# Turning residual tokens through VectorE and HBM instead of TensorE, with LayerNorm rows moved between the query's high parts

## What is computed

```python
# block 1: group norm, 1x1 convolutions to q, k, v, softmax attention, projection, residual
xn = group_norm(x); q, k, v = split(qkv_w @ xn + qkv_b)
x1 = x + proj_w @ (softmax(q^T k / sqrt(C)) applied to v) + proj_b
# block 2: on tokens t (N x C), LayerNorm, rows of length one, squared cosines, softmax
t  = tokens(x1);  z = layer_norm(t)
zn = z / |z|;     t = t + softmax((zn zn^T)^2) z
# block 3: LayerNorm, sign weights, clip to [-1, 1], seven levels, residual, back to channels
y  = layer_norm(t) @ (sign(W - mean W) * mean|W|) + b
out = channels(t + round(clip(y, -1, 1) * 7) / 7)
```

## Time and profile before

| | |
|---|---|
| Time, median of 3 runs | 1728.92 (1728.91, 1728.92, 1734.53) |
| Profiled execution, device time | 1734.94 |
| Its span | 1733.2 |
| Granted TensorE clock, mean | 0.995 |
| Busy: TensorE / VectorE / ScalarE / GpSimd | 96% / 79% / 57% / 45% |
| DMA queue of SyncE | 259.48 MB, 49.1% of 16 engines |

### The profile page before, as it was taken

One profiled execution on the slowest core, in us unless ns is written; L12 is line 12 of the kernel. 1 busy time (PEld: TensorE's weight loads), 2 busy tenths in 40 slices (PEclk: granted clock), 3 DMA queues, 4 the chain that ended last, 5 costly groups with the idle time before them and its releaser, 6 DMA issues.

```text
span 1733.2 us, 33604 instructions
## 1 busy us (share of the span) xinstructions
PE 1659.1 (96%) x10994; PEld 1509.8 (87%) x10994; DVE 1369.7 (79%) x2687; ACT 988.5 (57%) x1586; POOL 771.9 (45%) x1206
## 2 busy tenths in 40 slices
PE   7999999999999999999999999999999999999996
PEld 6897889988898898888988898898988989899886
DVE  6778688797877978788787887978778787887865
ACT  3455655656566565655657556565655656565572
POOL 1262634726345353543626346253553635337161
PEclk9999999999999999999999999999999999999998
DMA  4544546355454554545445463554545545463442
GB/s 127 163 121 155 147 140 194 117 170 151 148 173 130 184 146 155 145 148 186 140 153 155 143 190 112 179 154 148 162 141 174 159 139 154 149 188 103 161 132 61
DMA packets 218750, 259.86 MB, mean 150 GB/s; under 512 B 30176, under 2 KB 188256, under 8 KB 218720
## 3 DMA queue, kind: packets, MB, share of 16 engines
q1 hardware_dynamic: 218720, 259.48, 49.1%
HBM read 138.81 MB, written 120.59 MB: 150 GB/s over the span
## 4 chain that ended last, share of the span: by engine, by line
issue 24%; PE 18%; POOL 17%; DMA 15%; DVE 11%; ACT 7%; SPq 6%; POOLq 1%; DVEq 0%; ACTq 0%
DMA e_scratch<-x_norm 11%; PE wide L465 10%; SPq L392 6%; POOL e_back L1485 4%; ACT ln L863 4%; POOL prob L1480 3%; DMA e_back<-e_scratch 3%; PE turn L679 3%; POOL xn_lo L1436 2%; PE narrow L465 2%; POOL ln_r L1446 2%; DVE prob L1139 2%; DVE prob L1115 2%; POOL val L1472 2%; DVE neg_max L1125 1%
## 5 line engine op out<-in xcount | busy, mean ns | idle before, releaser
L465 PE MATMUL wide<-xn_hi,prob 128*128 128x512 f32 x1024 | 302.0, 399 | 21.2 <-DVE prob L1115 21.2
L822 ACT ACTIVATE expo<-wide,neg_max 128x1024 f32<-128x1024 f32 x128 | 142.7, 1114 | 199.4 <-DVE neg_max L1125 198.2
L465 PEld LDWEIGHTS wide<-xn_hi,prob 128*128 128x128 f32 x1024 | 187.3, 189 | 64.3 <-DVE prob L1115 24.5
L1496 POOL TENSOR_TENSOR carrier_p<-ones 128x1 f32<-128x1 f32 x60 | 15.7, 261 | 398.1 <-DVE y_sb L1241 395.6
L1139 DVE TENSOR_TENSOR prob<-e_back,prob 128x1024 fp32r<-128x1024 f32 x112 | 135.9, 1213 | 56.3 <-ACT prob L829 56.3
L1134 DVE STREAM_TRANSPOSE x_norm<-expo 128x1024 f32<-128x1024 f32 x112 | 139.3, 1244 | 44.5 <-ACT expo L822 42.6
L829 ACT ACTIVATE prob<-e_back 128x1024 fp32r<-128x1024 f32 x112 | 118.3, 1056 | 91.7 <-DMA e_back<-e_scratch 91.2
L1480 POOL TENSOR_TENSOR prob<-expo,prob 128x128 fp32r<-128x128 f32 (+6 forms) x112 | 146.2, 1317 | 47.6 <-DVE prob L1174 47.6
L465 PE MATMUL wide<-xn_lo,prob 128*128 128x512 f32 x512 | 161.2, 395 | 0.0
L1125 DVE TENSOR_REDUCE neg_max<-wide 128x1 f32<-128x1024 f32 x128 | 155.2, 1213 | 4.9 <-PE wide L465 3.6
L558 PE MATMUL wide<-prob 128*128 128x256 f32 x512 | 149.6, 292 | 5.0 <-DVE prob L1139 4.9
(11 more groups left out here) (181 smaller groups left out, 5180.7 us busy)
## 6 DMA issues: line engine op xcount, KB each, us to landing
e_scratch<-x_norm SPq DMA_DIRECT2D x112, 512.0 KB, 3.5
e_back<-e_scratch SPq DMA_DIRECT2D x448, 128.0 KB, 2.9
x_raw<-in_x SPq DMA_DIRECT2D x32, 512.0 KB, 3.7
e_back<-in_x SPq DMA_DIRECT2D x64, 256.0 KB, 5.0
out<-y_sb SPq DMA_DIRECT2D x64, 256.0 KB, 3.1
ln_scratch<-x_norm SPq DMA_DIRECT2D x30, 512.0 KB, 3.0
expo<-ln_scratch SPq DMA_DIRECT2D x120, 128.0 KB, 2.8
e_scratch<-x_norm SPq DMA_DIRECT2D x32, 448.0 KB, 2.6
```

What stands on the lines that cost most here:

```text
L465: mm = pe.matmul(o, lhsT, r, start=first and i == 0, stop=last and i == len(parts) - 1)
L822: act.activation(expo[:, n % DEEP], wide[n % 2][:, :], ACT.Exp, bias=neg_max[:, n:n + 1], accum_out=row_sum1[:, n:n + 1]).then_inc(e1_made, 1)
```

## The change

The tokens no longer go through TensorE. VectorE turns their 32 x 32 squares (`tok_turn`, two transposes of 128 x 512 for each half) into the place where the LayerNorm rows were, SyncE writes them to HBM and reads them back (`send_tok`, `fetch_tok`, between the sends and fetches of exponentials 1 and 2), and `output` adds them from SBUF in one instruction for each half. `turn_t` and its waits leave TensorE's front; behind the loop, the last sample keeps them (`output_last`). The bounds of the output move from VectorE (`clip`) to GpSimd (`quantise`). The LayerNorm rows: in `back` ScalarE makes four of the eight, and the other four in `front`, two behind each high part of the query; VectorE turns the first half in `back` and the second behind the first row maximum; GpSimd makes the first coefficients between two bias additions. On VectorE the group norm's sums go ahead of the query's low parts, the turned input tokens (`x_tokens`) behind them, and the low part of the last exponentials and one residual change places with their neighbours.

```diff
+        tok_scratch = nc.dram_tensor("tok_scratch", (2, P, N), F32).ap()
+        tok_in = tok_scratch.rearrange("h (q c) (b f) -> h b c q f", q=SQ, b=SQ)
...
+            def send_tok(f, hf):
+                sp.wait_ge(tok_turned, 2 * f + hf + 1)
+                sp.dma_start(tok_scratch[hf], tok_sent[hf]).then_inc(tok_written[hf], 16)
+            def fetch_tok(f, hf):
+                sp.wait_ge(tok_written[hf], 16 * (f + 1))
+                back = tok_back[hf].rearrange("p (q f) -> p q f", q=SQ)
+                for c in range(SQ):
+                    sp.dma_start(back[c * Q:(c + 1) * Q], tok_in[hf, c]).then_inc(tok_landed[hf], 16)
...
                 for n in range(SENT):
                     send(b, n)
+                    if f is not None and n in (1, 2):
+                        send_tok(f, n - 1)
                     fetch(b, n)
+                    if f is not None and n in (1, 2):
+                        fetch_tok(f, n - 1)
...  (TensorE)
-                if f is not None:
-                    pe.wait_ge(y_made, 4 * f + 4)
-                    turn_t(f, 0)
                 product1(b, 0)
                 scores1(b, 5)
-                if f is not None:
-                    pe.wait_ge(out_made, 2 * f + 1)
-                    turn_t(f, 1)
...  (ScalarE)
                 query_hi(b, 0)
+                if f is not None:
+                    layer_norm2(f, 4)
+                    layer_norm2(f, 5)
                 query_hi(b, 1)
+                if f is not None:
+                    layer_norm2(f, 6)
+                    layer_norm2(f, 7)
                 value_hi(b, 0)
                 value_hi(b, 1)
+                exp1(b, 0)
                 if f is not None:
                     ln2T_hi(f, 0)
-                exp1(b, 0)
...
-                for n in range(NT):
+                for n in range(HT):
                     layer_norm2(b, n)
...  (VectorE)
+            def tok_turn(f, hf):
+                dve.wait_ge(t2_made, NT * f + HT * (hf + 1))
+                dve.wait_ge(pv2_up, NT * f + NT)
+                for k in range(KC):
+                    last = dve.transpose(
+                        tok_sent[hf].rearrange("p (c k n t) -> p k n c t", c=SQ, k=KC, t=Q)[:, k],
+                        tok[:, HT * hf:HT * (hf + 1), tile(k)].rearrange("p n (c t) -> p n c t", t=Q))
+                last.then_inc(tok_turned, 1)
...
+            def output(f, hf):
+                dve.wait_ge(tok_landed[hf], 16 * SQ * (f + 1))
+                dve.wait_ge(q_made, 2 * f + hf + 1)
+                y = y_sb[:, hf].rearrange("p k (q f) -> p k q f", q=SQ)
+                dve.tensor_tensor(y, tok_back[hf].rearrange("p (q k f) -> p k q f", q=SQ, k=KC), y, ALU.add
+                                  ).then_inc(out_made, 1)
...
+                if more:
+                    gn_sums(b + 1, 0)
                 query_lo(b, 0)
+                if more:
+                    gn_sums(b + 1, 1)
+                query_lo(b, 1)
+                value_lo(b, 0)
...
                 x_tokens(b, 0)
-                query_lo(b, 1)
                 x_tokens(b, 1)
-                value_lo(b, 0)
+                row_max(b, 0)
+                if f is not None:
+                    ln2_turn(f, 1)
+                e1_turn(b, 0, f)
                 value_lo(b, 1)
-                if more:
-                    gn_sums(b + 1, 0)
-                row_max(b, 0)
+                row_max(b, 1)
                 if f is not None:
                     ln2T_lo(f, 0)
-                e1_turn(b, 0, f)
-                row_max(b, 1)
-                if more:
-                    gn_sums(b + 1, 1)
+                e1_turn(b, 1, f)
+                if f is not None:
+                    tok_turn(f, 0)
                 value_lo(b, 2)
-                e1_turn(b, 1, f)
                 value_lo(b, 3)
-                if f is not None:
-                    clip(f, 0)
                 row_max(b, 2)
                 if f is not None:
                     ln2T_lo(f, 1)
                 e1_turn(b, 2)
+                if f is not None:
+                    tok_turn(f, 1)
...
-                if f is not None:
-                    clip(f, 1)
...
+                e1T_last_lo(b)
                 e1T_lo(b, 6)
                 residual1(b, 4)
-                e1T_last_lo(b)
+                residual1(b, 5)
                 e2_hi(b, 0)
                 e2_hi(b, 1)
-                residual1(b, 5)
...
-                for hf in range(2):
-                    ln2_turn(b, hf)
+                ln2_turn(b, 0)
...  (GpSimd)
             def quantise(f, hf):
                 i = 2 * f + hf
+                aside(hf, y_made, 2 * i + 2)
+                pool.tensor_scalar(y_sb[:, hf], y_sb[:, hf], 1.0, -1.0, ALU.min, ALU.max).then_inc(clip_made, 1)
...
-                    for g in range(2):
-                        bias_quads(b + 1, g)
-                for g in range(N2):
+                    bias_quads(b + 1, 0)
+                layer_norm2(b, 0)
+                if more:
+                    bias_quads(b + 1, 1)
+                for g in range(1, N2):
                     layer_norm2(b, g)
```

More of the change, by code:

```diff
@@ L142, in build @@
         ln2_back = [expo[:, 2], expo[:, 3]]
+        tok_scratch = nc.dram_tensor("tok_scratch", (2, P, N), F32).ap()
+        tok_in = tok_scratch.rearrange("h (q c) (b f) -> h b c q f", q=SQ, b=SQ)
+        tok_sent = [ln2[:, HT * hf:HT * (hf + 1), :].rearrange("p n c -> p (n c)") for hf in range(2)]
+        tok_back = [tok[:, HT * hf:HT * (hf + 1), :].rearrange("p n c -> p (n c)") for hf in range(2)]
         e2_flat = x_tok[:, :, :].rearrange("p n c -> p (n c)")
@@ L278, in build @@
         ln2_landed = [sem("ln2_landed0"), sem("ln2_landed1")]
+        tok_turned = sem("tok_turned")
+        tok_written = [sem("tok_written0"), sem("tok_written1")]
+        tok_landed = [sem("tok_landed0"), sem("tok_landed1")]
         ln2T_up = sem("ln2T_up")
@@ L682, in ffn, with turn_t @@
                 mm.then_inc(y_up, 1)
-            def turn_t(f, hf, places=PLACES):
+            def turn_t(f, hf, places):
                 for k in range(KC):
@@ L1250, in quantise, with output_last @@
                                   ).then_inc(q_made, 1)
-            def output(f, hf, places=PLACES):
-                dve.wait_ge(tT_up, 2 * f + hf + 1)
+            def output(f, hf):
[4 more added lines that the diff above has]
+                                  ).then_inc(out_made, 1)
+            def output_last(f, hf, places):
+                dve.wait_ge(tT_up, hf + 1)
                 dve.wait_ge(q_made, 2 * f + hf + 1)
@@ L1269, in front @@
                 x_tokens(b, 0)
-                query_lo(b, 1)
                 x_tokens(b, 1)
-                value_lo(b, 0)
-                value_lo(b, 1)
-                if more:
-                    gn_sums(b + 1, 0)
                 row_max(b, 0)
                 if f is not None:
+                    ln2_turn(f, 1)
+                e1_turn(b, 0, f)
+                value_lo(b, 1)
+                row_max(b, 1)
+                if f is not None:
                     ln2T_lo(f, 0)
-                e1_turn(b, 0, f)
-                row_max(b, 1)
-                if more:
-                    gn_sums(b + 1, 1)
+                e1_turn(b, 1, f)
+                if f is not None:
+                    tok_turn(f, 0)
                 value_lo(b, 2)
-                e1_turn(b, 1, f)
                 value_lo(b, 3)
-                if f is not None:
-                    clip(f, 0)
                 row_max(b, 2)
@@ L1390, in _ @@
             quantise(f, 0)
-            output(f, 0, LAST)
+            output_last(f, 0, LAST)
             clip(f, 1)
             quantise(f, 1)
-            output(f, 1, LAST)
+            output_last(f, 1, LAST)
         @block.gpsimd
```

## The result

The changed kernel takes 1820.19 (median of four, 1816.35 to 1822.73) where the kernel before, now with a fourth run, takes 1729.69: a ratio of 1.0512, 95% interval 1.0487 to 1.0538, or 90 microseconds more. The profiled execution takes 1821.66 with a span of 1819.7; the profile of before has a span of 1733.2, so 86.5 are added.

What follows compares the result with a forecast made beforehand. SyncE's queue of dependent sends and fetches of exponentials, ending in T6, was taken to set the period. 0.96 + 3.23 + 0.4 = 4.6 a sample, 15 x 4.6 = 69, gave 1798 against the median 1728.92; range 1757 to 1840.

Steps and rivals of the forecast that it cites:

- second LayerNorm send: SyncE's send of the LayerNorm rows' second half, turned after the first row maximum: 13.9 after Q, now 9.0.
- Q: The start of a sample's queries on TensorE; the period runs from one to the next.
- first send: SyncE's first send of exponentials to HBM in a sample: at 781.8 against 780.84, +0.96.
- six steps: SyncE's queue from first to seventh send of exponentials: +3.23, plus 0.4 for waits on token writes.
- T6: End of VectorE's low part of the seventh turned block; each microsecond it comes late is one of the period.
- T6 - Q: Time from Q to T6 in a sample: to grow by 4.6, to about 65.5.
- rest: Period less T6 - Q, the time from T6 to the next Q: to stay 44.
- I take 0.2 each: Token fetches' waits for their own sends on SyncE's queue: 0.4 a sample, between nothing and 0.93 each.
- The price of the issues: Four more fetches on SyncE's queue in the second and third step each: 2 x 1.85 = 3.70.
- A: Rival: TensorE's work is the bound and gives back 3.06 a sample, 1683; chance 0.08.
- B: Rival: no change, VectorE takes TensorE's place as the bound, about 1729; chance 0.07.
- C: Rival: token trips crowd the DMA engines, 1847, and TensorE's clock falls too, 1871; chance 0.09.

Runs made afterwards that it cites:

- e7_early_second: e2_on_tensor with the second LayerNorm half turned behind the query's low parts, input tokens around the first maximum, exponentials' second low part ahead of the output: 1712.01, ratio 0.9888.
- e9_no_turn: e7_early_second with the tokens turned nowhere, so that the output adds them as they lie: 1739.91, ratio 1.0038.
- e1_no_trip: The changed kernel without the token sends and fetches through HBM and VectorE's wait for them; VectorE still turns the tokens: 1743.75, ratio 1.0084.
- The ladder: Three kernels compared: e1_no_trip 1743.75, e5_small 1771.91, the changed kernel 1820.19.
- e2_on_tensor: The changed kernel with tokens turned on TensorE as before and no trip through HBM; spread LayerNorm rows, new order and GpSimd bounds stay: 1740.11, ratio 1.0061.
- e3_trip_old_order: The changed kernel with LayerNorm rows, GpSimd's coefficients and VectorE's first orders as in the kernel before; the token trip stays: 1787.36, ratio 1.0319.
- e5_small: The changed kernel with every token DMA kept at its place but an eighth of the bytes moved: 1771.91, ratio 1.0241.

## Why the prediction was right, and where its sum was off

The direction, the place and the mechanism held; one term of the sum was too small. Step by step, eighth sample:

| step | forecast | measured |
|---|---|---|
| second LayerNorm send after Q | 13.9 | 13.85 |
| first send after Q | 18.38 | 18.38 |
| step from the first send to the second | 5.42 | 5.21 |
| second to third | 7.27 + 0.2 | 7.30 |
| third to fourth | 7.27 + 0.2 | 8.24 |
| fourth to fifth | 5.42 | 6.25 |
| fifth to seventh | 10.84 | 10.95 |
| six steps | 36.6 | 37.95 |
| seventh send to T6 | 10.43 | 10.36 |
| T6 - Q | 65.5 | 66.69 |
| T6 to the next Q | 44 | 43.88 |

**T6 sets the period.** Of the twelve kernels ten have a rest of 43.9 to 44.1, with T6 - Q from 60.8 to 67.6; the two others are `e7_early_second` and `e9_no_turn`, in which TensorE waits for T6 in two samples or fewer. But the constant rest alone doesn't say that T6 leads. In the kernel before TensorE waits for that low part 3 times, and in `e1_no_trip` 3 times too: there its own chain and T6 run level, and the sentence that a microsecond of T6 is a microsecond of the period holds only from some tenths on (T6 - Q grew by 5.91, the period by 5.77). In the changed kernel TensorE waits 15 times, and in the seven others of the ten in at least eight samples. The saving on TensorE turned into waits, as forecast: for the first scores it waits no more, for VectorE's last low part it waits 1.62.

**The token write was priced in the wrong place.** The step that failed is the one that ends at "I take 0.2 each, near the lower end, since the stretch is not full". The wait for the token's own write costs nothing, because the queue is busy with a fetch while it lands. But the bytes are on the engines when the next sends of exponentials go out: those are written 4.49 - 3.57 = 0.92 and 4.41 - 3.57 = 0.84 later. This is almost the 0.93 that the prediction held as the upper bound, and it fell on the sends behind, one step later each. The first step gave back 0.2, so the six came out 1.3 above the sum. The stretch was indeed not full, but it should have been judged with the new bytes in it. The kernel before, same view as above, in the stretch of its eighth sample that answers to 821 to 841:

```profile
786.00:791.00 5.00, 5.00 (x25) 4.05 (x24) 4.76 (x9) 2.67 (x5) 3.14 (x4) 1.00 0.59 185
791.00:796.00 5.00, 5.00 (x32) 4.36 (x31) 4.15 (x6) 3.49 (x5) 0.00 (x0) 1.00 0.59 191
796.00:801.00 5.00, 5.00 (x33) 4.40 (x32) 4.82 (x8) 2.27 (x3) 4.32 (x7) 1.00 0.55 182
801.00:806.00 5.00, 5.00 (x39) 4.77 (x38) 4.29 (x9) 1.65 (x3) 0.33 (x2) 1.00 0.69 210
```

A mean share of 0.605 is 12.1 of 20 microseconds. The two token halves, written and read, are 2.1 MB, which at the 284 GB/s worked out in the prediction take 7.4 of all engines: an estimate of 19.5 of 20, where the changed kernel then had a mean share of 0.91. That the stretch would be nearly full could be worked out from the trace of before.

**The price of the issues stood, while the bytes were there.** The sum has 3.70 for eight more issues, and in the changed kernel's queue they are all there: 3.70 + 0.92 + 0.84 is 5.46, the 5.4 that the trip costs. The ladder splits the same 5.4 as 2.2 + 3.2, because with few bytes the sends behind the issues are written sooner. So 0.4 for the bytes became 1.8 on top of the issues, and the forecast of 4.1 for the trip became 5.4. With the upper bound taken for the token writes the sum would have been 4.6 - 0.4 + 1.9 = 6.1, where 5.9 was measured. That upper end of the forecast, 1820, is the measured time to the microsecond by luck: the samples give less, and a difference between executions makes up for it.

**From samples to the kernel.** The samples 2 to 15 take 1682.80 - 128.7 = 1554.1 where they took 1473.7: 5.7 each, not 4.6. Over 15 samples that is 17 of the 22 by which the forecast of 1798 fell short. The rest is between executions: the two profiled ones differ by 86.7, the medians by 90.5.

**The rivals.** A (TensorE the bound) and B (VectorE the bound) needed a T6 that comes before TensorE or VectorE wants it, and would have shown in a rest above 44, as in `e7_early_second`; the changed kernel has 43.88. The Trainium skill's rule (Perfetto Trace Analysis, Identifying the Most-Contended Engine), to optimise first the engine with the highest occupancy, speaks for A; the runs disagree twice. With the transposes on TensorE (`e2_on_tensor`, 96%) the time is 1740, without them and without a trip (`e1_no_trip`) 1744; and even at 97% in `e7_early_second`, taking them away made it 1740 from 1712 (with a fall of the clock in it). C had the right mechanism, crowded DMA engines, at too high a price, and its second half did not matter: the clock does fall in the changed kernel (0.983 granted over the span, 0.995 before), but the rest behind T6 stays at 43.9. From the third sample to the fifteenth the falls lie 52 to 58 after Q, ahead of T6, in nine of thirteen; the four without one, the fourth, sixth, eighth and eleventh, have T6 - Q of 67.1, 66.7, 66.7 and 66.8, no less than the nine with one (66.5 to 68.3). The Trainium skill's price for a DMA (DMA: Bandwidth & Descriptors, Anatomy of one DMA, where it is fitted to DMAs that GpSimd issues) gave an estimate of 1772 and falls short. It has no term for other traffic, and here the same 512 KB took 2.64, 3.57, 4.49 and 6.03 from send to fetch, by what was ahead of it.

**Left open.** Why a first sample, which carries no tokens, also has its T6 2.8 later after Q than before (65.0 against 62.2) was not tried; it starts 2.9 earlier, so the end of its front is where it was, and it costs the whole kernel 0.7. It goes with the new order and not with the trip: it is 62.0 with the old order (`e3_trip_old_order`) and 65.5 without the trip (`e1_no_trip`).

## What to carry to other kernels

When a queue of dependent transfers sets the period, price a new transfer by what it does to those behind it, and judge the DMA engines' share with the new bytes counted in; another issuing engine or fewer issues hardly helped here once they were full (1811 and 1826 against 1820), while a pause in the queue took them nearly free (half of the trip moved there, half of the price gone). Taking work from an engine at 96% with a chain of waits beside it need not win anything: find the wait that ends last, check that the distance behind it is constant over the samples and that the busy engine does wait there, and shorten what leads to it. Here this meant keeping the spread LayerNorm rows and turning their second half four microseconds earlier than the change did.

## What the runs showed of the hardware

- A 512 KB write to HBM, from send to the fetch that waits for it: 2.64 with nothing ahead, 3.57 behind a fetch of as much, 4.4 to 4.5 behind a fetch of exponentials and one of tokens, 5.9 to 6.0 where the token fetch ahead is one straight DMA, 7.37 among transfers of a second queue.
- With four issues of small fetches between two sends, the next write took 2.87 instead of 3.57 (`e5_small`): here time of the issuing queue was also time for the DMA engines.
- In `e9_no_turn` a wait of 2.19 on a TensorE that had no other in the 15 microseconds before it was followed by 3.4 at a granted clock of 0.50. A fall like it stands in 13 of 15 samples, and in the two others the clock stayed at 1.00 behind 2.14 and 2.21. In the changed kernel's eighth sample it stayed at 1.00 behind a wait of 3.36 at the same place. Such a fall ahead of T6 cost the changed kernel nothing; `e9_no_turn` has less work than `e7_early_second` and is the slower one.
